# Fewer bytes written to a DRAM scratch tensor whose rows the reads repeat, and two fills moved from ScalarE to GpSimd

## What is computed

```python
qkv = h @ attn_w
q, k, v = jnp.split(qkv, 3, axis=-1)          # 16 heads of 8
q = q * cos + _rotate_half(q) * sin
k = k * cos + _rotate_half(k) * sin
scores = jnp.einsum('bqhd,bkhd->bhqk', q, k) / jnp.sqrt(jnp.float32(D))
scores = jnp.where(causal, scores, jnp.float32(-1e+30))
p = jax.nn.softmax(scores, axis=-1)
y = jnp.einsum('bhqk,bkhd->bqhd', p, v).reshape(B, T, C)
```

## Time and profile before

| | |
|---|---|
| timed runs, median | 341.47 us |
| lowest, highest | 338.66, 347.56 us |
| the profiled execution | 340.81 us |
| its span | 338.6 us |
| mean granted clock of TensorE | 0.993 of full speed |
| busy: PE, DVE, ACT, POOL | 315.3, 245.2, 220.0, 128.1 us |
| DMA issued through scr_qk | 12 writes of 384 KB, 16 reads of 288 KB |

### The profile page before, as it was taken

How to read it: one execution, slowest core, us unless ns; L and a number is a source line. 1 busy time by engine, 2 the same in 40 slices (tenths; PEclk the granted TensorE clock), 3 DMA queues, 4 the chain that set the end, 5 groups by cost and what they waited for, 6 DMA issues and landing times.

```text
span 338.6 us, 6802 instructions
## 1 busy us (share of the span) xinstructions
PE 315.3 (93%) x2270; PEld 220.6 (65%) x2270; DVE 245.2 (72%) x758; ACT 220.0 (65%) x649; POOL 128.1 (38%) x183
## 2 busy tenths in 40 slices
PE   8799989998989999999989998998999999999886
PEld 3348778665554433345446998985778687878675
DVE  4988875784898988888811552479788877887576
ACT  1488885375365756756676765754676667686995
POOL 3455564110641444410640440410685434535400
PEclk9999999999999999999998999999999999999999
DMA  7590000076763430091001003100100000000002
GB/s 213 196 274 10 2 0 2 8 243 170 209 206 89 113 102 3 1 326 52 5 31 56 2 31 111 33 1 2 54 20 15 0 2 1 3 0 0 2 0 65
DMA packets 21881, 22.47 MB, mean 66 GB/s; under 512 B 3894, under 2 KB 18646, under 8 KB 21846
## 3 DMA queue, kind: packets, MB, share of 16 engines
q1 hardware_dynamic: 18982, 16.78, 17.4%
q10 hardware_dynamic: 2352, 4.20, 3.7%
q0 software_dynamic: 512, 1.05, 1.0%
HBM read 14.22 MB, written 7.60 MB: 64 GB/s over the span
## 4 chain that ended last, share of the span: by engine, by line
PE 58%; DVE 16%; ACT 14%; issue 5%; POOL 4%; DMA 3%; SPq 0%; ACTq 0%; POOLq 0%
PE PS L1388 51%; PE PS L1442 5%; DVE PS L872 5%; ACT big L1167 5%; ACT big L1364 3%; POOL big L529 2%; DVE big L690 2%; DVE big L715 2%; DMA big<-in_A_WkT 2%; ACT big L1305 1%; ACT big L1141 1%; DMA XN<-scr_y,pos 1%; DVE XN L667 1%; ACT cw L1141 1%; PE PS L1704 1%
## 5 line engine op out<-in xcount | busy, mean ns | idle before, releaser
L1388 PE MATMUL PS<-big 128*128 128x128 f32 (+10 forms) x592 | 93.3, 308 | 7.0 <-DVE big L690 2.1
L1388 PEld LDWEIGHTS PS<-big 128*128 128x128 f32 (+3 forms) x592 | 56.2, 150 | 39.7 <-DVE mB L872 18.2
L529 POOL TENSOR_TENSOR big<-big,urec 128x1024 f32<-128x1024 f32 x24 | 45.6, 1900 | 60.2 <-DVE urec L722 45.4
L1167 ACT ACTIVATE big<-big 128x154 f32<-128x154 f32 x192 | 60.5, 319 | 10.6 <-DVE big L690 5.6
L872 DVE CUSTOM_DVE_ANT_0 PS<-PS,later 128x128 f32<-128x128 f32 (+3 forms) x128 | 60.1, 517 | 8.9 <-PE PS L1388 7.7
L1305 ACT ACTIVATE big<-PS 128x1024 f32<-128x1024 f32 (+3 forms) x64 | 43.2, 701 | 25.0 <-PE PS L1388 25.0
L1141 ACT ACTIVATE big<-PS 128x1280 f32<-128x1280 f32 (+2 forms) x30 | 32.3, 1088 | 27.0 <-PE PS L1442 24.5
L1388 PE MATMUL PS<-kkC,XT 128*128 128x462 f32 (+1 forms) x96 | 36.0, 511 | 1.9 <-DVE big L715 1.9
L1167 ACT ACTIVATION_READ_ACCUMULATOR big<-big 128x1 f32 x192 | 36.2, 189 | 0.0
L517 POOL TENSOR_TENSOR rstd<-ve,minus_half 128x4 f32<-128x4 f32 (+2 forms) x13 | 13.2, 1017 | 56.3 <-DVE ve L662 56.3
L1388 PEld LDWEIGHTS PS<-vwCm,big 128*128 128x128 f32 x256 | 30.8, 192 | 3.9 <-ACT big L1141 1.3
(11 more groups left out here) (192 smaller groups left out, 499.7 us busy)
## 6 DMA issues: line engine op xcount, KB each, us to landing
scr_qk<-big SPq DMA_DIRECT2D x12, 384.0 KB, 3.3
big<-scr_qk SPq DMA_DIRECT2D x16, 288.0 KB
big<-in_wv ACTq DMA_DIRECT2D x1, 2048.0 KB, 7.9
scr_x<-zrow SPq DMA_DIRECT2D x2, 448.0 KB, 6.9
scr_y<-big SPq DMA_DIRECT2D x2, 448.0 KB, 3.4
X<-in_x ACTq DMA_DIRECT2D x2, 256.0 KB, 3.3
big<-in_A_WoT ACTq DMA_DIRECT2D x1, 512.0 KB, 4.7
cw<-in_C_Wk SPq DMA_DIRECT2D x1, 512.0 KB, 5.2
```

The source lines that it names most:

```text
L529: pool.tensor_tensor(pn[:, 0:GH * P].rearrange("p (h k) -> p h k", h=GH), Pt[u % 3][:, :, 0:KM], r.to_broadcast([P, GH, KM]), ALU.mult).th ...
L1167: i = act.activation(Pt[u % 3][:, h, :], Pt[u % 3][:, h, :], ACT.Exp, accum_out=usum[:, u % 3, h:h + 1])
L1388: return pe.matmul(o, lhsT, rhs, start=start, stop=stop)
```

## The change

scr_qk now holds each of the three parts once, 24 rows of (part, dimension) for each of keys and queries, and not 72. A write goes to one place (128 KB). The reads make the repetition: for keys one DMA whose source has an extra outermost dimension of 3 with step 0, over 24 rows; for queries three DMAs, one for each part x, whose source repeats 8 rows three times. So a group of heads takes four reads, and PE waits for 64 counts in place of 32. The new instructions also join heads and tokens into one dimension by hand.

The ones and zeros beside sequence 0's values are written by POOL with two memsets, after its last splitting of sequence 1 and before `split_maxima(1)`, with a wait for ACT's folds up to F_VALUES (their weights lie in the same memory). For sequence 1 ACT still writes both, the ones now just before the zeros.

```diff
--- before.py
+++ after.py
@@ -240,7 +240,7 @@
         assert c.at <= BIGW, c.at
 
         PS = ctx.enter_context(nc.psum_tensor("PS", [P, 8, 512], F32))
-        scr_qk = nc.dram_tensor("scr_qk", (B, 2, SPLIT, HB, T), BF16, kind="Internal").ap()
+        scr_qk = nc.dram_tensor("scr_qk", (B, 2, 3, SPLIT // 9, HB, T), BF16, kind="Internal").ap()
         scr_x = [nc.dram_tensor(f"scr_x{b}", (SLOTS * P, D), F32, kind="Internal").ap() for b in range(B)]
         scr_y = [nc.dram_tensor(f"scr_y{b}", (SLOTS * P, D), F32, kind="Internal").ap() for b in range(B)]
 
@@ -468,17 +468,19 @@
             for b in range(B):
                 for a in range(3):
                     sp.wait_ge(part_ready[b], a + 1)
-                    sp.dma_start(scr_qk[b, 1].rearrange("(x y d) h t -> y (d h) x t", x=3, y=3)[a],
-                                 P3[:, 1, a, :].unsqueeze(1).to_broadcast([P, 3, T])).then_inc(scr_written[b], 16)
-                    sp.dma_start(scr_qk[b, 0].rearrange("(x y d) h t -> x (d h) y t", x=3, y=3)[a],
-                                 P3[:, 0, a, :].unsqueeze(1).to_broadcast([P, 3, T])).then_inc(scr_written[b], 16)
+                    for j in (1, 0):
+                        sp.dma_start(scr_qk[b, j, a].rearrange("d h t -> (d h) t"), P3[:, j, a, :]).then_inc(scr_written[b], 16)
                 if b:
                     store_maxima(0)
                 sp.wait_ge(scr_written[b], 16 * 6)
                 for g in range(HB // HG):
                     hs = slice(HG * g, HG * g + HG)
-                    sp.dma_start(ks[b][0:SPLIT, hs, :], scr_qk[b, 1, :, hs, :]).then_inc(stack_ready[b][g], 16)
-                    sp.dma_start(qs[b][0:SPLIT, hs, :], scr_qk[b, 0, :, hs, :]).then_inc(stack_ready[b][g], 16)
+                    parts = [scr_qk[b, j, :, :, hs, :].rearrange("a d h t -> a d (h t)") for j in range(2)]
+                    sp.dma_start(ks[b][0:SPLIT, hs, :].rearrange("r h t -> r (h t)"),
+                                 parts[1].unsqueeze(0).to_broadcast([3, 3, SPLIT // 9, HG * T])).then_inc(stack_ready[b][g], 16)
+                    for x in range(3):
+                        sp.dma_start(qs[b][SPLIT // 3 * x:SPLIT // 3 * (x + 1), hs, :].rearrange("r h t -> r (h t)"),
+                                     parts[0][x].unsqueeze(0).to_broadcast([3, SPLIT // 9, HG * T])).then_inc(stack_ready[b][g], 16)
                     if b and g == 0:
                         store_maxima(1)
             for c in range(2, N_CHUNK):
@@ -585,6 +587,10 @@
             pool.wait_ge(part_ready[1], 2)
             pool.tensor_tensor(P3[:, :, 2, :], qk, P3[:, :, 1, :], ALU.subtract).then_inc(part_ready[1], 1)
             pool.wait_ge(part_ready[1], 3)
+            pool.wait_ge(preC_act, sum(j[2] for j in PREC[:F_VALUES]))
+            v = vaug[:, 0].rearrange("p t h m -> p (t h) m")
+            pool.memset(v[:, :, HDB:HDB + 1], 1.0).then_inc(v_ready, 1)
+            pool.memset(v[:, :, HDB + 1:32], 0.0).then_inc(v_ready, 1)
             split_maxima(1)
 
             def scatter(b):
@@ -1236,10 +1242,10 @@
             def values(b):
                 v = vaug[:, b].rearrange("p t h m -> p (t h) m")
                 copy(v[:, :, 0:HDB], XN[:, QT * b:QT * b + QT, :].rearrange("p t (h d) -> p (t h) d", h=HB)).then_inc(v_ready, 1)
-                copy(v[:, :, HDB:HDB + 1], ones[:, 0:QT * HB].unsqueeze(2)).then_inc(v_ready, 1)
 
             def no_values(b):
                 v = vaug[:, b].rearrange("p t h m -> p (t h) m")
+                copy(v[:, :, HDB:HDB + 1], ones[:, 0:QT * HB].unsqueeze(2)).then_inc(v_ready, 1)
                 copy(v[:, :, HDB + 1:32], ones[:, 0:32 - HDB - 1].unsqueeze(1).to_broadcast([P, QT * HB, 32 - HDB - 1]),
                      0.0).then_inc(v_ready, 1)
 
@@ -1253,7 +1259,6 @@
             copy_C(F_LN, F_VALUES)
             act.wait_ge(preC_act, sum(j[2] for j in PREC[:F_VALUES]))
             values(0)
-            no_values(0)
             copy_C(F_VALUES, F_MAX)
             copy_maxima(0)
             copy_C(F_MAX, len(PREC))
@@ -1638,7 +1643,7 @@
             def scores_for_maximum(m):
                 hp, qt = divmod(m, QT)
                 if m % M_CHUNK == 0:
-                    pe.wait_ge(stack_ready[0][m // M_CHUNK], 32)
+                    pe.wait_ge(stack_ready[0][m // M_CHUNK], 64)
                 if m >= 3:
                     pe.wait_ge(s_max, m - 2)
                 for j in range(2):
@@ -1652,7 +1657,7 @@
                 hp, qt = divmod(n, QT)
                 w = (qt + 1) * P
                 if n % M_CHUNK == 0:
-                    pe.wait_ge(stack_ready[b][n // M_CHUNK], 32)
+                    pe.wait_ge(stack_ready[b][n // M_CHUNK], 64)
                 if k < 2:
                     pe.wait_ge(s_max, M0)
                 else:
```

## The result

| | before | after |
|---|---|---|
| timed runs of this comparison, median | 347.44 us (6 runs, 338.66 to 347.93) | 361.71 us (6 runs, 360.72 to 362.66) |
| the profiled execution, and its span | 340.81, 338.6 us | 361.89, 360.1 us |
| mean granted clock | 0.993 | 0.962 |
| begin of step 0, 4, 8, 12 | 106.78, 116.52, 125.92, 135.32 | 111.26, 123.26, 144.71, 157.69 |

The ratio is 1.064, 95% interval [1.058, 1.070]: slower, as forecast, and 363.0 us was forecast for a measured 361.71.

A forecast was written before the change was run, and what follows sets the result against it. The prediction took PE, 58% of the chain, as the bound. Step 8 19.0 us later through confined reads, ACT's 1.0 us gain swallowed, plus 3 us of clock made 22 on 340.81: 363 us, range 348 to 396.

The forecast's parts named there:

- The fills: Ones and zeros of sequence 0: 1.0 us gained before the vwCm copy, POOL's 1.5 us of memsets hidden.
- The engines: Stack reads from scr_qk: source count 3 confines them to three engines, 31 us per sequence at 25.5 GB/s each.
- slow engines: Rival for the stack reads: each of three engines runs at 17.2 GB/s, +52 us, 393 us; chance 0.25.
- destination decides: Rival for the stack reads: destination rows set 12 engines, no confinement, 339.8 us; chance 0.08.
- in part: Rival for the stack reads: keys keep 12 engines, only queries use three, 345 us; chance 0.07.
- Who waits: Stores of maxima land behind the reads: step 0 at 111.3, step 4 at 121.2, step 8 at 144.9, +19.0 us.
- small stores pass the backlog: Rival for the stores of maxima: they pass the reads, step 0 keeps its time, 340 us; chance 0.05.
- SP itself: SP's queue: sixteen read issues instead of eight, 0.3 to 0.6 us each, hidden under the transfers.
- The clock: Half clock after PE idles before steps 0 and 8: some 1.5 us per stretch, twice, 3 us.

The follow-up runs named there:

- e1_fills: The kernel before with only the fills of sequence 0's ones and zeros moved to POOL, scr_qk as before: 339.64 us, ratio 0.996.
- e3_pad: The kernel before with scr_qk padded from 3 x 24 to 3 x 25 rows, so the reads' source counts 3 outermost: 369.34 us, ratio 1.083.
- e5_half: The kernel after with the keys of a group read by three plain DMAs of 24 rows, only queries by the repetition: 348.48 us, ratio 1.022.
- e4_actq: The kernel after with the stores of maxima issued by ACT, right behind its copy of the maxima, instead of SP: 368.51 us.
- e7_turns: The kernel after with each later quarter of sequence 1's reads behind the next store of maxima in SP's queue: executions of 344.80, 345.88, 352.71 and 355.58 us.
- e6_hold: The kernel after with 52 matmuls, whose results nobody reads, on PE ahead of the wait at step 8: 357.53 us.
- e2_wide: The kernel after with key parts stored once, query parts twice, and six plain reads of 24 rows a group, no zero step: ratio 1.001.
- e4b_ctrl: The kernel before with the stores of maxima issued by ACT instead of SP: 373.48 us.

## Why the prediction was right, and where its steps were not

**The fills.** Forecast 1.0 us gained on the path and POOL's 1.5 us hidden. The memsets took 1.36 us for the zeros (near the lower bound of 1.3) and end 1.5 us behind the subtraction (98.72 to 100.22); e1_fills shows 0.9 us at step 0. Right, and swallowed in the kernel after, as said.

**The engines.** I took the smaller side for a transfer whose sides differ, 3 engines at 25.5 GB/s. The trace has a share of 0.19 to 0.20 and 76 to 81 GB/s; e3_pad has the same with 72 rows on the other side. The Trainium skill's page "DMA: Bandwidth & Descriptors", section "Why a DMA increments its semaphore by 16 and not by 1", has the rule of the largest count up to 16 that divides both sides; the traces agree for 3 against 72 and 3 against 24. These pairs can't tell that rule from mine of the smaller side. The rival "slow engines" (393 us) falls with the rate: each of the three ran at 26 GB/s, so the 17.2 GB/s of the old steady state is not what one engine can do. What held the twelve to it no run shows. The rivals "destination decides" and "in part" fall with the share; e5_half is the partial case built on purpose, and took 348.5 us where I had written 345.

**Who waits.** Forecast step 0 at 111.3, 4 at 121.2, 8 at 144.9; measured 111.26, 123.26, 144.71. The landing of the third maxima, 12.5 us, decided. But the sentence under it, that transfers on one engine pass in order, was too broad: in e4_actq a store is complete 4.7 us after its issue through the same full engines from another queue. The rival "small stores pass the backlog" was wrong for this kernel because the stores share SP's queue, not because engines never let them pass. e7_turns says it from the other side. Step 4 came late for another reason than the one I gave: its maxima landed at about 121.7 (issued by 117.3, 4.4 us to landing), near the forecast 121.2, but PE, at half clock since step 0, reached step 4 only at 123.26 and did not wait.

**SP itself.** I wrote that the sixteen issues, at 0.3 to 0.6 us each, are hidden. They grew: 5.07 and 6.53 us for three reads and 8.03 us for six writes, and my reading, which no run tested by itself, is that SP cannot hand over a transfer while the queue of the three engines is full. That made the writes and the first store of maxima late in a way I did not foresee. It did not change the sum, because the same backlog then lay in SP instead of the engines and drained at the same rate (share 0.20 to 0.21 and 78 to 82 GB/s from 119 to 131 us); in e3_pad, with three times the bytes to write, step 0 came 7.6 us later than in the change.

**The clock.** The term was "some 1.5 us per such stretch, twice: 3 us". The sum was close by luck and the split wrong. The half-clock stretches last not 3.4 us as in the earlier trace rows but some 10 and 17 us (about 109.5 to 119.3 and 136.3 to 153.3). Behind the first wait, steps 0 to 4 took 12.0 us instead of 9.74, but those 2.3 us were hidden in the wait for step 8. Behind the second, steps 8 to 12 took 12.98 instead of 9.40: 3.6 us, and e6_hold, which keeps PE busy there, gives 4.2 back.

Together: step 8 later by 18.8 (forecast 19.0), 3.6 of clock (forecast 3), 0.9 less in the rest, makes 21.5 us of span against a forecast of 22. The 0.9 was not foreseen. The kernel before had its half-clock stretch at 177 us, where these eight matmuls took 1.94 us; the kernel after has none at that place, and the same eight, at 199.56, took 1.07.

## What to carry to other kernels

When a read is rewritten with a repetition of step 0, look at what now stands outermost on either side: a count of 3 there cost 21.5 us here, and the bytes saved were bytes that nobody waited for. Before giving up such a layout, look at the queue: the bulk was in time for its own readers, and three 4 KB stores behind it in the same queue cost 17 us with the clock that followed, which three lines of order gave back. And put nothing on an engine that stands on the chain (ACT here) only to get a second queue, without a control that prices its issues.

## What was not expected of the hardware

- An issue on SP is not a fixed cost. Reads of 0.68 to 0.73 us for one and 2.1 us for three took 5.07 and 6.53 us for three when the backlog lay on three engines, and one write in e3_pad took 8.00 us. With the reads on more engines (e2_wide, sequence 0) each took 0.32 to 0.37 us, but for one of 1.36.
- The half-clock level (0.50, which is 1.2 GHz) lasted long after a wait: PE idled 5.62 us before step 0 and 11.98 us before step 8, and the clock was down from 109.5 to 119.3 and from 136.3 to 153.3. It also came where PE had no such wait, as in the profiled execution of e2_wide between steps 0 and 8 and in e4b_ctrl, and it is not settled here what released it there.
- Twelve engines together moved the stack reads at 206 GB/s, 17 each; three moved them at 78, 26 each. Confinement by a factor of four cost a factor of 2.6 in rate. The twelve were not always at 206: in e2_wide, with the same share of 0.79, they moved 161.
